# A second raw buffer for the experts' w2, gathered rows centred instead of normalised, and a new order for the end of attention

## The reference, cut to what matters

```
x: (8, 16, 16, 256) f32                       8 images of 256 tokens, 2048 tokens in all
z = ln(x)                                     over channels, eps 1e-6
q, k, v = z Wq^T + bq, z Wk^T + bk, z Wv^T + bv
r = softmax(q k^T - dist/(2 sigma^2)) v       within the token's row of 16
c = softmax(q k^T - dist/(2 sigma^2)) v       within the token's column of 16
x = x + (r + c) Wo^T + bo
t = ln(x)                                     eps 1e-5
gates = softmax(t wg); top-1 expert of 8; place in the expert = running count; capacity 256
out = x + gate * relu(t w1[e]) w2[e]          w1: 8 x 256 x 1024, w2: 8 x 1024 x 256
                                              a token past the capacity keeps x alone
```

## Time and profile before

| what | value |
|---|---|
| three runs | 199.15, 200.94 and 201.48 us; median 200.94 us |
| profiled execution, first to last instruction | 199.3 us; the page gives no other time of it |
| PE busy | 179.9 us (90%) |
| PEld, DVE | 171.8 us (86%), 135.9 us (68%) |
| ACT, POOL | 117.1 us (59%), 120.7 us (61%) |
| mean granted TensorE clock | 0.968 of full speed |

### The profile page before, as it was taken

The page is one execution under the profiler, slowest core; times in us unless marked ns, Lnnn a source line. Parts: engine busy times, 40 slices in busy tenths (PEclk is TensorE's granted clock), DMA queues, the critical chain, the costliest instruction groups (busy, mean ns, idle before and its releaser), DMA issues.

```text
span 199.3 us, 3920 instructions
## 1 busy us (share of the span) xinstructions
PE 179.9 (90%) x1356; PEld 171.8 (86%) x1356; DVE 135.9 (68%) x417; ACT 117.1 (59%) x284; POOL 120.7 (61%) x153
## 2 busy tenths in 40 slices
PE   7599999799999989889996992799999999999990
PEld 7499889699999978669996991799999999999980
DVE  0477999999999997618577718629659486675510
ACT  2347876677875875744788338257493866827000
POOL 3324976195686665575629618648595876918351
PEclk9979999999999999999999999579999999999997
DMA  5799992021131122754961290941926729161010
GB/s 189 217 393 346 266 348 101 33 101 63 58 107 55 58 106 68 246 199 144 311 225 50 61 360 0 312 164 21 355 101 205 269 42 366 71 211 43 3 64 26
DMA packets 23829, 31.67 MB, mean 159 GB/s; under 512 B 2696, under 2 KB 20617, under 8 KB 23808
## 3 DMA queue, kind: packets, MB, share of 16 engines
q1 hardware_dynamic: 21232, 26.32, 40.6%
q0 software_dynamic: 1616, 4.24, 5.9%
q10 hardware_dynamic: 960, 0.85, 1.3%
HBM read 23.02 MB, written 8.55 MB: 158 GB/s over the span
## 4 chain that ended last, share of the span: by engine, by line
PE 51%; DMA 14%; DVE 13%; issue 6%; POOL 6%; ACT 5%; SPq 3%; POOLq 1%; DVEq 0%; ACTq 0%
DMA sl<-slots 5%; PE banks_v L587 5%; PE banks_v L581 5%; PE banks_v L580 5%; PE banks_o L649 4%; DMA wg_sb<-in_L_ffn_wg 3%; PE bank_q L587 3%; DMA w_in_sb<-in_L_ffn_w 3%; PE bank_q L580 3%; PE bank_q L581 3%; ACT w_high L901 2%; PE bank_pT L587 2%; PE bank_pT L580 2%; PE bank_pT L581 2%; POOL w_low L521 2%
## 5 line engine op out<-in xcount | busy, mean ns | idle before, releaser
L521 POOL TENSOR_TENSOR w_low<-w_in_sb,w_high 128x1024 fp32r<-128x1024 f32 x15 | 35.9, 2418 | 10.3 <-ACT w_high L901 10.3
L901 ACT ACTIVATE w_high<-w_in_sb 128x1024 fp32r<-128x1024 f32 x30 | 30.3, 1052 | 6.0 <-DMA w_in_sb<-in_L_ffn_w 6.0
L540 POOL DMA_INDIRECT out<-y,goal x16 | 16.0, 1002 | 18.5 <-issue 8.4
L473 POOL DMA_INDIRECT slots<-row,slot x14 | 14.1, 1010 | 13.6 <-DVE slot L1179 11.1
L1268 DVE TENSOR_TENSOR w_low<-w_in_sb,w_high 128x1024 fp32r<-128x1024 f32 x12 | 18.7, 1591 | 3.0 <-ACT w_high L901 2.8
L649 PE MATMUL banks_o<-v_sb,pT 128*128 128x266 f32 x64 | 16.3, 396 | 0.9 <-ACT pT L867 0.8
L580 PE MATMUL banks_v<-w_high,h_high 128*128 128x256 f32 x64 | 16.0, 287 | 0.0
L1002 ACT ACTIVATE exp_g<-shift_g,rstd_g 128x8 f32<-128x8 f32 x16 | 4.7, 292 | 19.1 <-DVE shift_g L1248 19.1
L581 PE MATMUL banks_v<-w_high,h_low 128*128 128x256 f32 x64 | 15.7, 283 | 0.0
L580 PE MATMUL bank_xT<-xg_high,w_high 128*128 128x256 f32 x32 | 9.3, 310 | 7.0 <-DVE w_low L1268 5.1
L1276 DVE SCALAR_TENSOR_TENSOR h_low<-bank_s,h_high 128x512 fp32r<-128x512 f32 x8 | 5.5, 690 | 14.5 <-ACT h_high L1013 14.5
(11 more groups left out here) (251 smaller groups left out, 658.3 us busy)
## 6 DMA issues: line engine op xcount, KB each, us to landing
w_in_sb<-in_L_ffn_w SPq DMA_DIRECT2D x16, 1024.0 KB, 7.5
sl<-slots SPq DMA_DIRECT2D x9, 266.0 KB, 4.5
slots<-empty SPq DMA_DIRECT2D x8, 266.0 KB, 7.3
out<-row SPq DMA_DIRECT2D x7, 256.0 KB, 2.1
sl<-in_x SPq DMA_DIRECT2D x4, 256.0 KB, 6.1
sl<-in_x SPq DMA_DIRECT2D x2, 512.0 KB, 9.2
table_in<-in_tables SPq DMA_DIRECT2D x1, 292.0 KB, 6.2
w_in_sb<-in_L_conv_Wk SPq DMA_DIRECT2D x1, 256.0 KB, 3.5
```

The source lines that it names most:

```text
L473: nc.gpsimd.indirect_dma_start(slot_rows, bass.IndirectOffsetOnAxis(ap=slot_of(i)[:, t:t + 1].bitcast(u32), axis=0), row_of(i)[:, t, :], N ...
L521: step = nc.gpsimd.tensor_tensor(w2_low[e % 2][:, half, :], w2_in_sb[:, half, :], w2_high[e % 2][:, half, :].bitcast(f32), ALU.subtract)
L540: nc.gpsimd.indirect_dma_start(out_rows, bass.IndirectOffsetOnAxis(ap=goal[j][:, c:c + 1].bitcast(u32), axis=0), y[j][:, c, :], None, boun ...
L901: nc.scalar.activation(high[e % 2][:, half, :], raw[:, half, :], ACT.Copy).then_inc(ready, 1)
```

## The change

- **Buffers.** `xb` and `v_sb` of attention become parts of one tile `vx`, and `vx` serves as a second raw w2 buffer once attention is over: `w2_raw = [w2_in_sb, vx]`, taken in turn by the expert's number.
- **Loads.** w2 of expert 1 is loaded as soon as image 7's residual is done, ahead of the loads of `slots`; w2 of expert e waits for the split of expert e-2 instead of e-1. w1 of expert 2 is loaded right after image 5's store, ahead of the early load. Image 6's store moves behind the landing of the early load.
- **Experts.** On ACT and DVE the two halves of w1's split for expert e+2 stand between the first quarters of hidden(e+1), and ACT's split of w2 stands at the turn's end; the first two turns have an order of their own, in which the first half of w2 of expert 1 is split between quarters of hidden(0).
- **Rows centred.** Rows are only centred ahead of w1; relu lets a positive factor through, so the inverse root is multiplied into the gate after the product (`ginv`, `gate_g`). `gathered` no longer waits for POOL, and the late squares and `late_rstd` go.
- **End of attention.** PE transposes image 6's probabilities ahead of image 7's scores, takes the values of image 7 by token tile, each with its transpose behind it, and runs attention_out(7, 0) ahead of image 6's count. On DVE the residual of image 6, tile 0, goes ahead of the weights of image 7, tile 0, and the residual of image 7, tile 0, ahead of image 6's place. The one-hots of image 6 are made on POOL, which then converts its slots and scatters after the early load has landed.

The diff, cut:

```diff
+        vx = sb("vx", [P, 4 * (MW + VW)])
+        xb = [vx[:, 4 * MW + 2 * VW * j:4 * MW + 2 * VW * (j + 1)].rearrange("p (t r) -> p t r", t=2) for j in range(2)]
+        v_sb = [vx[:, 2 * MW * j:2 * MW * (j + 1)].rearrange("p (t r) -> p t r", t=2) for j in range(2)]
+        w2_raw = [w2_in_sb[:, :, :], vx[:, 0:FC * D].rearrange("p (c d) -> p c d", c=FC)]
...
-            for i in range(EARLY):
+            for i in range(EARLY - 1):
                 store_x2(i)
+            sp.wait_ge(x2_ready, 2 * EARLY)
+            sp.dma_start(out_view[:, tiles(EARLY - 1), :], row[1][:, :, 0:D]).then_inc(x2_stored[1], 16)
+            sp.wait_ge(w1_split, 2)
+            sp.dma_start(w1_in_sb[:, :, :], w1_view[2]).then_inc(w1_in, 16)
+            for j in range(2):
+                sp.wait_ge(row_sent[j], 32 * (EARLY // 2))
             sp.dma_start(sl_early, slots_view[:, 0, :, :]).then_inc(early_in, 16)
+            sp.wait_ge(early_in, 16)
             sp.wait_ge(x2_ready, 2 * (B - 1))
             sp.dma_start(out_view[:, tiles(B - 2), :], row[0][:, :, 0:D]).then_inc(x2_stored[0], 16)
-            sp.wait_ge(early_in, 16)
-            sp.wait_ge(w1_split, 2)
-            sp.dma_start(w1_in_sb[:, :, :], w1_view[2]).then_inc(w1_in, 16)
+            sp.wait_ge(x2_ready, 2 * B)
+            sp.dma_start(w2_raw[1], w2_view[1]).then_inc(w2_in[1], 16)
...
-            sp.wait_ge(w2_split, 1)
-            sp.wait_ge(first_w2_low, 1)
-            sp.dma_start(w2_in_sb[:, :, :], w2_view[1]).then_inc(w2_in, 16)
-
             sp.sem_inc(y_free, 2)
             for e in range(2, E):
-                sp.wait_ge(w2_split, e)
-                sp.dma_start(w2_in_sb[:, :, :], w2_view[e]).then_inc(w2_in, 16)
+                sp.wait_ge(w2_split, e - 1)
+                if e == 2:
+                    sp.wait_ge(first_w2_low, 1)
+                sp.dma_start(w2_raw[e % 2], w2_view[e]).then_inc(w2_in[e % 2], 16)
...
+            pool.wait_ge(placed, 1)
+            pool.wait_ge(place_in, 16)
+            for t in range(2):
+                nc.gpsimd.tensor_scalar(onehot[0][:, t, :], place_row, place_of[0][:, t:t + 1], None, ALU.is_equal).then_inc(first_onehot_ready, 1)
+            nc.gpsimd.tensor_copy(slot_of(B - 2)[:, :], place_of[0][:, :]).then_inc(cast_ready, 1)
+            pool.wait_ge(cast_ready, 1)
+            pool.wait_ge(early_in, 16)
             scatter_rows(B - 2)
             scatter_rows(B - 1)
...
+                if part == 1 or e == 0:
+                    step.then_inc(w2_split, 1)
...
             slot_rstd(0, 2)
+            split_w2(1, [0])
             slot_rstd(2, 3)
             for j in range(2):
                 pool.wait_ge(x2_stored[j], 16 * (B // 2 - j))
             pool.wait_ge(x2_stored_last, 16)
             scatter_y(0)
-            split_w2(1, range(2))
+            split_w2(1, [1])
...
+            transpose_prob(B - 2)
             scores(B - 1)
             counts(B - 3)
-            transpose_prob(B - 2)
             attention_out(B - 2, 0)
             attention_out(B - 2, 1)
-            values(B - 1)
-            transpose_prob(B - 1)
+            values(B - 1, [0])
+            transpose_prob(B - 1, [0])
+            values(B - 1, [1])
+            transpose_prob(B - 1, [1])
+            attention_out(B - 1, 0)
             counts(B - 2, late=True)
-            attention_out(B - 1, 0)
             attention_out(B - 1, 1)
             keep_warm(WARM_TAIL, ps_pT)
...
+            def last_values(t):
+                act.wait_ge(v_made, B + t)
+                wait(act, pre_ready, B - 2)
+                nc.scalar.activation(v_sb[(B - 1) % 2][:, t, :], ps_v[:, t, 0:MW], ACT.Copy).then_inc(v_ready, 1)
+
+            transposed_prob(B - 2)
             split_w2(0, which=[1])
-            transposed_prob(B - 2)
             exponentials(B - 1)
-            values(B - 1)
             for t in range(2):
+                last_values(t)
                 transposed_prob_tile(B - 1, t)
...
+            def centred(rows, target, t):
+                return nc.scalar.activation(target[:, t, :], rows[:, t, 0:D], ACT.Identity, bias=rows[:, t, COL_MEAN:COL_MEAN + 1])
             act.wait_ge(xT_made, B)
             for t in range(2):
                 act.wait_ge(x2_ready, 2 * (B - 2) + t + 1)
-                squares(0, row[0], xn, t)
+                centred(row[0], xn, t).then_inc(xn2_ready, 1)
             for t in range(2):
                 act.wait_ge(x2_ready, 2 * (B - 1) + t + 1)
-                squares(1, row_last, s_col, t)
+                centred(row_last, s_col, t).then_inc(xn2_ready, 1)
             act.dma_start(out_view[:, tiles(B - 1), :], row_last[:, :, 0:D]).then_inc(x2_stored_last, 16)
-            act.wait_ge(nmr_t_ready, 1)
-            for t in range(2):
-                late_rows(0, row[0], xn, t).then_inc(xn2_ready, 1)
             act.wait_ge(early_in, 16)
             for t in range(2):
-                squares(2, sl_early, xs[0], t)
-            act.wait_ge(nmr_t_ready, 2)
-            for t in range(2):
-                late_rows(1, row_last, s_col, t).then_inc(xn2_ready, 1)
-            act.wait_ge(nmr_t_ready, 3)
-            for t in range(2):
-                step = late_rows(2, sl_early, xs[0], t)
+                step = centred(sl_early, xs[0], t)
...
-            hidden(0, range(4))
+            hidden(0, [0, 1])
+            split_w2(1, which=[0])
+            hidden(0, [2, 3])
+            split_w1(2, which=[0])
             slot_squares(1, 1)
-            split_w1(2, which=[0])
+            gathered_T(1)
             slot_squares(0, 2)
+            split_w1(2, which=[1])
             slot_exps(1, 1)
-            gathered_T(1)
             slot_exps(0, 2)
-            split_w1(2, which=[1])
+            hidden(1, [0, 1])
             slot_squares(2, 3)
-            hidden(1, [0, 1])
-            split_w2(1)
             hidden(1, [2, 3])
             gathered_T(2)
+            split_w2(1, which=[1])
             slot_squares(3, 4)
             for e in range(1, E - 1):
-                if e + 1 < E:
-                    slot_exps(e + 1, e + 2)
-                hidden(e + 1, [0, 1])
-                split_w2(e + 1)
+                hidden(e + 1, [0])
+                if e + 2 < E:
+                    split_w1(e + 2, which=[0])
+                slot_exps(e + 1, e + 2)
+                hidden(e + 1, [1])
+                if e + 2 < E:
+                    split_w1(e + 2, which=[1])
                 hidden(e + 1, [2, 3])
                 if e + 2 < E:
                     gathered_T(e + 2)
-                    split_w1(e + 2)
+                split_w2(e + 1)
                 if e + 3 < E:
                     slot_squares(e + 3, e + 4)
...
             maxima(B - 1, 0)
             place(B - 3, slot_of(B - 3)).then_inc(slot_ready, 1)
             maxima(B - 1, 1)
+            residual(B - 2, 0)
             weights(B - 1, 0)
-            residual(B - 2, 0)
             residual(B - 2, 1)
             weights(B - 1, 1)
             choose(B - 2)
-            route.mark(place(B - 2, place_of[0]))
             residual(B - 1, 0)
-            route.done()
-            dve.wait_ge(place_in, 16)
-            onehots(0)
+            route.done(place(B - 2, place_of[0]))
+            dve.sem_inc(placed, 1)
             residual(B - 1, 1)
             choose(B - 1)
             route.done(place(B - 1, place_of[1]))
+            dve.wait_ge(place_in, 16)
             dve.wait_ge(pT_made, 2 * B)
-            onehots(1)
-            for n in range(2):
-                nc.vector.tensor_copy(slot_of(B - 2 + n)[:, :], place_of[n][:, :]).then_inc(slot_ready, 1)
+            for t in range(2):
+                nc.vector.tensor_scalar(onehot[1][:, t, :], place_row, place_of[1][:, t:t + 1], None, ALU.is_equal).then_inc(onehot_ready, 1)
+            nc.vector.tensor_copy(slot_of(B - 1)[:, :], place_of[1][:, :]).then_inc(slot_ready, 1)
...
-                    step = nc.vector.tensor_scalar(xs[e % 2][:, t, :], sl[:, r, 0:D], rstd_g[:, r:r + 1], nmr_g[:, r:r + 1], ALU.mult, ALU.add)
+                    step = nc.vector.tensor_scalar(xs[e % 2][:, t, :], sl[:, r, 0:D], sl[:, r, COL_MEAN:COL_MEAN + 1], None, ALU.add)
...
+                gate.done(nc.vector.tensor_tensor(gate_g[:, tiles(e)], ginv[:, tiles(e)], rstd_g[:, tiles(e)], ALU.mult))
...
             hidden_low(0, [1, 2, 3])
+            gathered(1)
             slot_shift(1)
             slot_shift(0)
-            gathered(1, 1)
             split_w1(2, which=[0])
             gathered_low(1)
+            gathered(2)
             split_w1(2, which=[1])
+            hidden_low(1, [0, 1])
             output_rows(0, 2)
-            gathered(2, 3)
-            hidden_low(1)
+            hidden_low(1, [2, 3])
             gathered_low(2)
             for e in range(1, E - 1):
                 slot_shift(e + 1)
                 if e + 2 < E:
-                    gathered(e + 2, e + 3)
-                    hidden_low(e + 1)
```

(12 more changed lines are left out.)

75 lines of the change are left out of this document (25 added, 50 removed).

## The result

| kernel | runs | median | range |
|---|---|---|---|
| before | 5 | 201.25 us | 199.15 to 201.68 |
| changed | 5 | 192.69 us | 190.79 to 195.86 |

The ratio is 0.957, with a 95% interval of 0.948 to 0.965: the change makes the kernel 3.5 to 5.2% faster. The forecast was 190.7 us in 187.5 to 195.5, and faster. The ratio leaves out the changed kernel's two slowest runs, 195.86 and 195.66 us, which lie over 1.5% above its fastest; the medians of all runs have the same ratio. In every run whose span is on record the device time is 1.8 to 2.0 us more than the span. The profiled run is the changed kernel's slowest, 195.86 us with a span of 194.0; the others span 188.9 to 193.8.

A forecast was written before the change was run, and what follows sets the result against it. PE's hole before hidden(3), bound by the single raw w2 buffer and ACT's order: -5.28 - 2.75 - 2.0 - 0.35 + 1.0 = -9.4 us, span 199.3 to 189.9; median forecast 190.7 us, 8 in 10 range 187.5 to 195.5.

The forecast's parts named there:

- The hole and its slow stretch: PE's idle time before hidden(3) goes, -5.28 us, and the half-speed clock behind it, -2.75 us.
- T: Time from the start of gather_T(3), the end of hidden(2), to the span's end: 84.97 us before, forecast 77.94.
- Rival B: New hole in the experts, from POOL's w2 split or a loop of w1's reload: 194 to 197 us, chance 0.13.
- Rival C: Same reload loop but longer, PE waiting over about 4 us at hidden(4) to (7): 209 us, slower, chance 0.04.
- The last expert: Before expert_out(7), PE waits for w2's split, now behind all four quarters on ACT: +1.0 us.
- The end of attention: Reordered products, residuals and one-hots bring hidden(0) from 87.58 to 85.6: -2.0 us.
- hidden(0) to the end of hidden(2): The first two turns rearrange behind earlier scatters and slots loads: 26.4 us instead of 26.75, -0.35.
- M: Time from hidden(0)'s start to the start of gather_T(3), the end of hidden(2): 26.75 us before, forecast 26.4.
- the front: From the transposes of image 5's probabilities to hidden(0)'s start: 23.03 us before, forecast 21.03.
- rival A: The front gives nothing, hidden(0) starting at 87.6 as before: 192.7 us, up to 194, chance 0.13.
- the signs that I had named: Included no PE idle above 2 us from hidden(0) to expert_out(6), and clock 1.00 from 20 us to the last slice.
- the w1 split as PE's last releaser: Sign in the experts: each expert's w1 split was forecast never to be last before hidden.

The follow-up runs named there:

- one_raw_w2: The changed kernel with one raw w2 buffer, w2(1) loaded behind the slots loads, and the new order of experts 2 to 7 kept: 237.73 us, ratio 1.181.
- old_turn_order: The changed kernel with ACT's and DVE's old order of a turn for experts 2 to 7, both raw w2 buffers kept: 195.74 us.
- w2_load_late: The changed kernel with w2(1)'s load behind the eight slots loads and its first half split after hidden(0): 191.73 us, ratio 0.963.
- slot2_last: slot2_alone plus ACT's split of expert 7's w2 moved ahead of quarters 2 and 3 of hidden(7): 191.7 us, ratio 0.957.
- second batch: Later runs on another chip, the changed kernel beside its variants; the changed kernel itself took 196.4 us there, ratio 0.974.
- slot2_alone: The changed kernel with a semaphore of its own for expert 2's slots load: 191.86 us, beside 196.4 for the changed kernel on the same chip.

## Why the prediction was right, and where it missed

**The hole and its slow stretch: right.** Forecast -5.28 and -2.75, with +1.0 at the last expert: T down by 7.03. Measured 84.97 to 77.86, 7.11. The buffer is the cause: without it the hole is in every turn (one_raw_w2), and with it there is none under the old order of a turn (old_turn_order) or with w2(1) late (w2_load_late). The load of w2(2) was issued at 96.14 and never seen on the chain. Rival B's loop does not close: no wait at hidden(3) to (7) in any trace with two buffers. Rival C's five waits do exist, in the kernel with one buffer.

**The last expert: right**, 0.8 us instead of 1.0, 0.75 to 0.98 in the eight other traces that keep ACT's new order and both buffers, by the mechanism named: PE starts 0.1 us after POOL's pair ends (182.58 and 182.48 in the changed kernel), and 0.5 us of the wait went when ACT's split moved ahead.

**The end of attention: direction right, size 2.0 against 1.44.** Less 0.56 us, by which image 5's transposes were later than before's, attention_out(7, 0) came at 76.8 (forecast 76.6), dispatch(0, 0) at 80.3 (80.0), image 7's count at 81.2 (80.9), DVE's one-hots at 82.2 (81.7), dispatch(1, 0) at 82.7 (82.1), the early product at 84.5 (83.85) and hidden(0) at 86.1 (85.6). Half of the 0.56 is there by dispatch(0, 0), and it isn't the one-hots of 0.94 instead of 0.61: the dispatch stood behind the `keep_warm` products, as it did with the one-hots on DVE. The other half is mainly two handovers that I priced below the rows of before. From the count to DVE's one-hots I had 0.8 us; it took 0.99, and 0.98 before. From there to dispatch(1, 0) I had 0.4; it took 0.50 in both kernels. Of the causes of the gain the order carries 0.4 us and the centred rows the other 1.0: both waits that the kernel before had for normalised rows, 0.45 us ahead of dispatch(0, 0) and 0.3 ahead of the early product, are gone with the old order as well. I had looked at the second alone.

**hidden(0) to the end of hidden(2): this step failed.** I wrote that the scatters would start at 82.3, the last land near 89.2, and the `slots` loads shift by 2.4 us. It landed at 91.8, 2.6 us late: 0.57 from the later start, 0.6 at POOL's first scatter (the early rows landed 0.15 later than the start accounts for, and it began 0.84 us after them and not 0.4), 0.5 in the issue of the four (the first took 1.53 us), and 0.95 because the last landed 3.95 us after its issue, beside w2(1)'s megabyte, where I had let it take 3.0. SP issued the loads at 91.86, no sooner than the 91.56 of the earlier trace rows. I had named w2(1)'s megabyte as running beside these scatters and then asked only who waits for the megabyte, not what it does to them. The collision of POOL and DVE I did foresee, and let `gathered_low(2)` slip to 106.5; it came at 108.55. M was 29.44 instead of 26.4: 3.0 of the 4.1 us by which the span missed. When the tie falls the other way M is 26.03, better than forecast, and that is luck of the run and no merit of the forecast: it had no tie in it.

**The rest of the miss** is 0.57 us of a later start and 0.56 of the front, less 0.08 gained in T. And one reading was wrong: I took the profiled span of 199.3 us for a time at the low end of before's runs. The runs of all kernels are 1.8 to 2.0 us longer than their spans, so 199.3 is a run of about 201.2, at the median; 189.9 of span should have been read as 191.8 us, 0.9 under the median measured. The median of 192.69 is also what rival A gave (192.7), but not by A's way: hidden(0) came 0.9 us sooner than before and not at the same time. Of the signs that I had named, the idle time above 2 us and the clock below 1.00 in the middle did come; the w1 split as PE's last releaser did not.

**A better kernel** than the changed one isn't shown by the medians within a chip: slot2_last 191.7 against 192.47, with the intervals of their ratios 0.952 to 0.962 and 0.952 to 0.963. In the second batch, on another chip, slot2_alone led by 4.5 us with intervals that touch. What the traces show is that expert 2's semaphore takes the `slots` landing out of the tie: M is 26.03 or 26.04 in all four with it or with w2(1) late, against 26.03 to 30.59 in the others with two buffers. DVE's lead over POOL is then 0.08 us, small but the same in both traces (0.08 and 0.09), since both engines start from ACT's work.

## What to carry to other kernels

A second buffer is worth what the chain load, split, reload is longer than a turn, and an order that leans on it can cost far more than it gives once the buffer is gone: undo them separately. When a large load is moved ahead of small ones, ask who is waiting for what lands beside it, and not only who waits for the load. If a kernel's times scatter by 2%, look for a tie between two engines or queues in its trace, and separate what waits for one load from what waits for eight.
